# A selective-scan kernel on one core: the scaling of the next u is split between GpSimd (one sequence) and ScalarE (the other)

## The reference: what is computed

```
delta = softplus(xp[..., :R] @ dt_proj_w.T + dt_proj_b);  A = -exp(A_log)
def step(h, inp):                       # h: (2, 512, 128)
    dt, bt, ct, xt = inp
    h = exp(dt[:, :, None] * A) * h + (dt * xt)[:, :, None] * bt[:, None, :]
    y = einsum('bdn,bn->bd', h, ct)
    return (h, y)
x = layernorm(x + (y + x * D_param) @ out_proj_w.T)
x = layernorm(x + (silu(x @ w_gate.T) * (x @ w_up.T)) @ w_down.T)
```

## Time and profile before

| | |
|---|---|
| median of 3 runs | 2700.8 us (2699.85 to 2701.7) |
| profiled execution, its own time | 2700.41 us |
| its span, first to last instruction | 2698.6 us |
| DVE busy | 2607.0 us, 97% |
| PE busy | 2339.9 us, 87% |
| ACT busy | 1524.0 us, 56% |
| POOL busy | 1219.6 us, 45% |
| mean granted TensorE clock | 0.961 of full speed |

### The profile page before, as it was taken

The page is one execution under the profiler, slowest core; times in us unless marked ns, Lnnn a source line. Parts: engine busy times, 40 slices in busy tenths (PEclk is TensorE's granted clock), DMA queues, the critical chain, the costliest instruction groups (busy, mean ns, idle before and its releaser), DMA issues.

```text
span 2698.6 us, 48060 instructions
## 1 busy us (share of the span) xinstructions
PE 2339.9 (87%) x17036; PEld 1288.4 (48%) x17036; DVE 2607.0 (97%) x4160; ACT 1524.0 (56%) x1929; POOL 1219.6 (45%) x1317
## 2 busy tenths in 40 slices
PE   7866677999789987899879998799977998899998
PEld 4322224555345543455435553455534554465567
DVE  5999999999999999999999999999999999999892
ACT  5554355664666455664556646666466655654643
POOL 3444444444444444444444444444444444444430
PEclk8999999999899999999999999999989999999899
DMA  4656665777667776678767786577766877688694
GB/s 152 208 210 218 219 234 210 274 270 272 240 209 278 279 262 235 232 280 279 263 211 249 278 286 246 205 265 279 274 240 209 278 281 262 240 288 305 228 359 153
DMA packets 192058, 672.15 MB, mean 249 GB/s; under 512 B 20944, under 2 KB 26064, under 8 KB 191824
## 3 DMA queue, kind: packets, MB, share of 16 engines
q1 hardware_dynamic: 152432, 544.02, 56.9%
q10 hardware_dynamic: 39392, 125.06, 13.5%
HBM read 660.61 MB, written 8.39 MB: 248 GB/s over the span
## 4 chain that ended last, share of the span: by engine, by line
PE 41%; DVE 36%; issue 12%; ACT 10%; DMA 1%; POOL 0%; ACTq 0%; DVEq 0%; POOLq 0%
DVE h L681 18%; DVE banks L661 12%; PE banks L1159 10%; PE banks L995 10%; PE banks L1235 9%; PE banks L1135 8%; DVE h L678 5%; ACT a L953 5%; ACT L692 1%; PE banks L1087 1%; PE banks L1083 1%; PE banks L1099 1%; ACT dt L720 0%; PE banks L1143 0%; ACT v L834 0%
## 5 line engine op out<-in xcount | busy, mean ns | idle before, releaser
L953 ACT ACTIVATE a<-banks 128x2048 f32<-128x2048 f32 x512 | 961.4, 1878 | 857.9 <-PE banks L1159 703.7
L661 DVE TENSOR_TENSOR banks<-a,h 128x512 f32<-128x512 f32 x2048 | 1346.8, 699 | 3.3 <-ACT a L953 3.3
L681 DVE SCALAR_TENSOR_TENSOR h<-u_bc,BCt,banks 128x512 f32<-128x512 f32 x1496 | 1040.1, 732 | 1.9 <-PE banks L1235 1.9
L553 POOL TENSOR_TENSOR dexp<-spread,dt 128x512 f32<-128x512 f32 x512 | 538.7, 1052 | 654.7 <-DVE banks L661 612.1
L1235 PE MATMUL banks<-h,cz 128*32 128x512 f32 x4096 | 708.5, 625 | 113.6 <-DVE h L681 99.9
L1159 PE MATMUL banks<-dexp,A 32*128 32x256 f32 x8192 | 617.3, 417 | 123.7 <-ACT a L953 122.7
L1159 PEld LDWEIGHTS banks<-dexp,A 32*128 32x128 f32 x8192 | 386.8, 193 | 458.8 <-ACT a L953 305.0
L566 POOL TENSOR_SCALAR u_bc<-u_bc,BCt 128x512 f32<-128x512 f32 x552 | 376.8, 695 | 401.6 <-DVE banks L661 389.5
L995 PE MATMUL banks<-vT,w_ring 128*128 128x256 f32 x1792 | 448.3, 393 | 7.6 <-ACT up L920 6.9
L995 PEld LDWEIGHTS banks<-vT,w_ring 128*128 128x128 f32 x1792 | 323.1, 190 | 174.8 <-issue 119.2
L678 DVE TENSOR_TENSOR h<-u_bc,banks 128x512 f32<-128x512 f32 x552 | 351.2, 674 | 15.9 <-PE banks L1235 9.5
(11 more groups left out here) (176 smaller groups left out, 1230.2 us busy)
## 6 DMA issues: line engine op xcount, KB each, us to landing
u_bc<-u_scratch SPq DMA_DIRECT2D x1021, 512.0 KB, 4.6
w_ring<-in_gu_w ACTq DMA_DIRECT2D x112, 512.0 KB, 5.2
w_ring<-in_down_w ACTq DMA_DIRECT2D x56, 512.0 KB, 5.5
a<-in_gu_w ACTq DMA_DIRECT2D x16, 512.0 KB, 13.0
a<-in_down_w ACTq DMA_DIRECT2D x8, 512.0 KB, 4.5
x_tok<-in_x_rows SPq DMA_DIRECT2D x15, 256.0 KB, 5.9
out_rows<-v ACTq DMA_DIRECT2D x15, 256.0 KB, 4.4
U<-in_xT ACTq DMA_DIRECT2D x7, 512.0 KB, 5.1
```

Source lines behind the costliest of these rows:

```text
L553: e.tensor_tensor(dexp[:, q % E_RING, :, :, :], spread[:, :].unsqueeze(1).unsqueeze(1).to_broadcast(shape), by_step[:, :, first:first + BS ...
L661: e.tensor_tensor(m_ps[:, b, :], a[:, blk % A_RING, b, s, :], h[:, (t - 1) % H_RING, b * D:(b + 1) * D], ALU.mult).then_inc(s_m, 1)
L681: e.scalar_tensor_tensor(h[:, t % H_RING, part], u_bc[:, t % U_RING, part], BCt[c % 2][:, 0, b * TB + tl:b * TB + tl + 1], m_ps[:, b, :], ...
L953: e.activation(dst.rearrange("p b t (x j) -> p x (b t) j", j=GP), src.rearrange("p g (i r j) -> p (g i) r j", i=PAIR, j=GP), ACT.Exp, scal ...
```

## The change

At the same places (all but the last of them, position 1022: 275 are left) GpSimd multiplies u by B only for sequence 0. For sequence 1 ScalarE does it, two positions ahead of the use, right behind the exponential of that even position (`scale(t + 2, 1)`), by an ACTIVATE Copy with B as its scale; but only where the stages which the timetable puts on the two positions t and t + 1 have together at most `LIGHT` = 16 of the load that `LOAD` gives each stage: these are 233 of the 275 places. At the other 42, DVE's second sum is again the SCALAR_TENSOR_TENSOR. The semaphore s_z becomes two, s_zp (GpSimd's) and s_za (ScalarE's), and DVE waits for u's transfer itself at every position.

```diff
@@ -33,6 +33,10 @@
 WT = 2 * KB * P
 TILES = HB + 2 * KB
 SLOTS = 2
+
+LOAD = {"sq": 24, "root": 16, "gate": 8, "mask": 5, "xpc": 2, "pre": 6, "soft": 40, "utc": 4, "ymc": 4, "ln1": 36, "vtc": 4,
+        "act": 10, "dnc": 2, "ln2": 36}
+LIGHT = 16
 HB_RING = 4
 TILES_14 = 3
 TILES_IN_A = 16
@@ -315,7 +319,7 @@
         d_w15 = [sem(f"d_w15_{i}") for i in range(TILES_IN_A)]
         s_const, s_ident, s_zero, s_spread, s_gates, s_A = (
             sem(s) for s in ("s_const", "s_ident", "s_zero", "s_spread", "s_gates", "s_A"))
-        s_z = sem("s_z")
+        s_zp, s_za = sem("s_zp"), sem("s_za")
         s_work = sem("s_work")
 
         s_dexp, s_p, s_exp, s_cz, s_m, s_h, s_y, s_ycp = (
@@ -346,10 +350,20 @@
         turns, norms = {}, {}
 
 
-        scaled = [t + 1 for t in range(FIRST_U, SEQ - 1, 2) if not any(
-            stage in PIECES for slot in range(SLOTS * (t % TB - 1), SLOTS * (t % TB + 1))
-            for stage, _, _ in plans[t // TB].get(slot, ()))]
-        scaled = {t: BATCH * i for i, t in enumerate(scaled)}
+
+        def at_steps(t, steps):
+
+            return [(stage, j) for step in range(max(t, 0), t + steps) for slot in (SLOTS * (step % TB), SLOTS * (step % TB) + 1)
+                    for stage, _, j in plans[step // TB].get(slot, ())]
+
+        def light(t):
+            return sum(LOAD.get(stage, 0) for stage, _ in at_steps(t, 2)) <= LIGHT
+
+        even = range(FIRST_U - 1, SEQ - 4, 2)
+        on_pool = {(t + 2, 0): i for i, t in enumerate(
+            t for t in even if not any(stage in PIECES for stage, _ in at_steps(t, 2)))}
+        on_act = {place: i for i, place in enumerate(
+            (t + 2, 1) for t in even if (t + 2, 0) in on_pool and light(t))}
         for c in range(CHUNKS + 1):
             if c == CHUNKS:
                 first_tail = len(turns)
@@ -561,10 +575,8 @@
                 if tl < 4 and c:
                     e.wait_ge(s_work, emptied("xp", c, 0))
                 e.wait_ge(d_u[slot], 16 * (t // U_RING + (slot >= FIRST_U)))
-                for b in range(BATCH):
-                    part = u_bc[:, slot, b * D:(b + 1) * D]
-                    e.tensor_scalar(part, part, BCt[c % 2][:, 0, b * TB + tl:b * TB + tl + 1], 1.0, ALU.mult, ALU.mult
-                                    ).then_inc(s_z, 1)
+                part = u_bc[:, slot, 0:D]
+                e.tensor_scalar(part, part, BCt[c % 2][:, 0, tl:tl + 1], 1.0, ALU.mult, ALU.mult).then_inc(s_zp, 1)
 
             for q in range(DEXP_AHEAD):
                 diagonals(q)
@@ -581,7 +593,7 @@
                                 e.wait_ge(s_m, BATCH * (t + 1))
                             piece_before(e, x, stage, j)
                             piece_behind(e, x, stage, j)
-                    if t + 1 in scaled:
+                    if (t + 1, 0) in on_pool:
                         e.wait_ge(s_m, BATCH * (t + 1))
                         scale(t + 1)
 
@@ -660,7 +672,7 @@
                         e.wait_ge(s_h, BATCH * (t - 1) + b + 1)
                     e.tensor_tensor(m_ps[:, b, :], a[:, blk % A_RING, b, s, :],
                                     h[:, (t - 1) % H_RING, b * D:(b + 1) * D], ALU.mult).then_inc(s_m, 1)
-                if t >= FIRST_U and t not in scaled:
+                if t >= FIRST_U:
                     e.wait_ge(d_u[t % U_RING], 16 * (t // U_RING + (t % U_RING >= FIRST_U)))
                 if t >= H_RING:
                     e.wait_ge(s_y, t - H_RING + 1)
@@ -673,8 +685,11 @@
                         e.wait_ge(s_ucp, BATCH * t + b + 1)
                     e.wait_ge(s_m, BATCH * t + b + 1)
                     part = slice(b * D, (b + 1) * D)
-                    if t in scaled:
-                        e.wait_ge(s_z, scaled[t] + b + 1)
+                    if (t, b) in on_pool or (t, b) in on_act:
+                        if (t, b) in on_pool:
+                            e.wait_ge(s_zp, on_pool[t, b] + 1)
+                        else:
+                            e.wait_ge(s_za, on_act[t, b] + 1)
                         e.tensor_tensor(h[:, t % H_RING, part], u_bc[:, t % U_RING, part], m_ps[:, b, :], ALU.add
                                         ).then_inc(s_h, 1)
                     else:
@@ -963,6 +978,14 @@
                                         y_ps[:, part].rearrange("p (g i j) -> p g i j", i=PAIR, g=G), ACT.Copy)
                 last.then_inc(s_ycp, 1)
 
+            def scale(t, b):
+                c, tl, slot = t // TB, t % TB, t % U_RING
+                if tl < 4 and c:
+                    e.wait_ge(s_work, emptied("xp", c, 0))
+                e.wait_ge(d_u[slot], 16 * (t // U_RING + (slot >= FIRST_U)))
+                part = u_bc[:, slot, b * D:(b + 1) * D]
+                e.activation(part, part, ACT.Copy, scale=BCt[c % 2][:, 0, b * TB + tl:b * TB + tl + 1]).then_inc(s_za, 1)
+
             first_chunk()
             for t in range(SEQ):
                 c = t // TB
@@ -978,6 +1001,8 @@
                 for i in range(SLOTS):
                     if SLOTS * t + i in EXP_AT:
                         exponents(EXP_AT[SLOTS * t + i], p_ps)
+                    if i == 0 and (t + 2, 1) in on_act:
+                        scale(t + 2, 1)
                     for stage, x, j in plans[c].get(SLOTS * (t % TB) + i, ()):
                         behind(x, stage, j)
                         before(x, stage, j)
```

## The result

The changed kernel takes 2756.8 us (median of 4 runs, 2748.73 to 2757.97) against 2701.25 us: ratio 1.0199, 95% interval 1.0186 to 1.0212. The forecast was 2722 us with the upper end at 2740: the direction was right, the size was not, +55 us where +21 were worked out. The execution shown here took 2757.86 us, span 2756.1.

The account below looks back on a forecast made before the run. DVE, busy for 97% of the span, was taken as the bound for nearly all the scan. The terms -19.5 + 25.5 + 11 + 0.6 + 4 = +21.6 us on 2700.4 gave 2722 us, range 2702 to 2740.

Parts of the forecast that it names:

- DVE's own instructions: DVE's scan: products 0.08 us shorter at 275 places, sums 0.06 us longer at 42; together -19.5 us.
- eight stretches: DVE's second sums near chunk starts and positions 970 to 988 wait for ScalarE's late scaled u: 25.5 us before growth.
- 11 of growth: Six later chunk starts: delayed PE-ScalarE chain plus DVE arriving sooner add 1.8 us each, 11 us.
- places like 254: Places just in time before the change become 0.7 us late, in six chunks 4 us.
- As load it is hidden: ScalarE's 233 ACTIVATEs, 168 us, fit into its 1175 us to spare; only their date counts.
- two hand-overs: ScalarE's L895 and L720, for which PE stands: a new instruction ahead of each delays the chain, 1.3 us a stretch.
- the 25.5 read from the trace of before: DVE's waits for scaled u, without growth: 4.3 us first chunk, six later starts 2.4 to 3.6 each, last 3.
- its 0 to 6: Last chunk, around position 984: DVE's net wait for scaled u, taken as 3 us, between 0 and 6.
- Worse: Chain delays continue beyond the stretches, with twice the growth and all 6 us of the last chunk: +40, 2740; chance 0.10.
- ScalarE is in time: ScalarE's lateness belongs to that execution's slow phases; only DVE's own terms act: 2681 us; chance 0.08.
- full block: DVE's products lose the whole overlap with GpSimd by the Trainium skill's rule, gaining 60 us: 2684; chance 0.01.
- Late, but no growth: ScalarE's additions vanish in its idle time, the last chunk gives all back: +3 us, 2704; chance 0.13.

Follow-up runs that it names:

- experiment 2: Changed kernel without ScalarE's scaling places, GpSimd's one instruction released by DVE's first sum instead of the products: ratio 1.0032 to the kernel before.
- experiment 1: Changed kernel without ScalarE's scaling places, DVE multiplying sequence 1 itself everywhere: 2693.17 us, ratio 0.9953; run again 2699.07 us, 0.9994.
- experiment 6: Changed kernel with ScalarE scaling only at the 105 in-time places: 2707.77 us, ratio 1.0014; second run, only the other 128: 2748.99 us, 1.0165.
- experiment 7: Changed kernel with LIGHT = 0, ScalarE scaling only at 122 places without any load of stages: 2720.41 us, ratio 1.0076.
- Experiment 3: Changed kernel with three dependent 128x1 copies on ScalarE instead of each scaling; DVE waits for none, multiplies sequence 1 itself: 2717.57 us, ratio 1.0046.
- 9: Behind the slot's stages: changed kernel with ScalarE's copies nobody waits for, 2699.65 us, 0.9987; with scaling at only the 105 in-time places, 2698.11 us, 0.9978.
- experiment 8: Changed kernel with ScalarE's scaling behind the stages of its slot instead of ahead of them: 2716.72 us, ratio 1.0065.
- experiment 5: Changed kernel with ScalarE's scaling ahead of the exponential of its position instead of behind it: 2737.35 us, ratio 1.0112.

## Why the prediction was wrong in size

- **DVE's own instructions: right.** 275 x 0.08 = 22 us of gain: experiment 2 gives 275 x 0.07 = 19 by the row and 18.8 by the sum over the scan; its ratio gives 21 us against experiment 1's first run and 10 against the second. The 0.06 us a sum stand in the rows. Alone, GpSimd's half with DVE multiplying sequence 1 everywhere should give -5.5 us: measured -13 and -2. The rule of the Trainium skill (SBUF — State Buffer, "Who interferes with whom") that the later one is fully blocked does not hold in size here: 0.20 us of overlap by the recorded spans cost 0.07, and the measurement decides. The profile calls its spans on GpSimd rough, so part of the difference can lie in them; no run here tells.
- **DVE waits for ScalarE's scaled u in eight stretches, at positions 8 to 10, 16 to 45 of each later chunk, and 968 to 988: right in place**, by L693's row and the timeline. The rule LIGHT looks at the wrong thing: experiments 6 and 7. The size was wrong in the six chunk starts: there DVE stands 63.8 us longer than before, forecast 33 (18 as it was, 11 of growth, 4 at places like 254). The first chunk gave 2.0, not 4.9, and the last 6.5, not 3.
- **"As load it is hidden": the step that failed.** It went into the sum as nothing outside the stretches, and as 1.3 us in each for two hand-overs. Experiment 3 shows 14 to 24 us for the load without any date, 9 that most of it goes when the instruction stands behind the stages. Of the 72 us by which DVE stood longer, 36.9 go by that move alone (97.7 - 60.8 in experiment 8's trace). The prediction had 15.6 us for all growth and 31 as its bound. It had two hand-overs in a stretch, 1.3 us; PE's waits for ScalarE grew by 3.2 to 4.2 us in each chunk, the one before L1112 among them. The late x of experiments 3 and 6 is hardly part of it: in the third to seventh chunks of the changed kernel x lands 9.6 to 10.3 us behind DVE's start in three and 5.5 and 7.0 in two, and from four positions ahead of that start to 64 behind it DVE stands 11.6 to 12.1 us in the three and 11.4 and 11.5 in the two.
- **The remaining 35 us** (60.8 - 25.7) answer to the 25.5 read from the trace of before plus 4 for places like 254 (0.4 to 0.5 us each in experiment 8, 0.7 forecast; in the changed kernel 1.0 to 2.6, in all 9.2), and are 6 above them. The last chunk gave 6 us net there too (20.6 against 14.3), the upper end of its 0 to 6.
- **Rivals.** "Worse" had the right mechanism, delays handed on along the chain of PE and ScalarE, and at 2740 it too was 17 us short. "ScalarE is in time" and "full block" fell. "Late, but no growth" (2704) is what experiment 8 comes nearest to (2716.72).
- **Open.** With the same program the stretches differ. In experiments 3 and 6 DVE stands longest in the chunks in which x lands latest (over 11 us behind DVE's start), and these have the lowest granted clock over their first 20 positions (0.80 to 0.84, against 0.91 to 0.96 in the third to seventh otherwise). Whether PE is late there because x is, or because of the clock, was not tried apart. In experiment 1's first trace x lands at 8.9 and 9.4 us in two chunks and DVE stands for nothing in them, at a clock of 0.99, so landings as late as that cost nothing there. How much of the load's cost in experiment 3 came by the hand-overs and how much by the issue of x is open too: both fall when it stands behind the stages. Why experiment 1 gave two ratios is not shown either; its runs differ in their mean clock, and 0.9953 and 0.9994 lie on both sides of 0.9978.

## What to carry to other kernels

An engine that is 56% busy is not free for work with a date: read from its timeline how late it is against its own place in the program, position by position, since decoupled engines hide lateness until someone waits for them. Put added work behind the hand-overs of its slot, not ahead of them: here instructions of 0.7 us ahead of evacuations made TensorE wait 3 to 4 us longer in each chunk, though ScalarE was 44% idle. When two offloads are in one change, time each alone: here GpSimd's half was worth 2 to 13 us, and ScalarE's cost 54 to 66. Here load and date together cost more than the sum of the two alone.

## What the runs showed of the hardware that I had not expected

- A GpSimd TENSOR_SCALAR that reaches, by the recorded spans, 0.20 to 0.22 us into a DVE TENSOR_TENSOR with two SBUF operands makes it 0.07 to 0.08 us longer, no more; sums with one operand in SBUF and one in PSUM, with the same instruction under them, cost 1.32 us a pair, 1.31 without.
- TensorE's granted clock over a chunk's first 20 positions lay between 0.80 and 0.96 in one execution of one program, while its work there was the same (experiment 6).
- The same 512 KB transfer of x took 3.7 us from issue to landing in one chunk (experiment 5) and 9.0 in another (experiment 7).
